# Graph layer on one core: routed groups 7 of 24 instead of 1 of 4, in seven slot tiles of two 64-row strips with 448 nodes each, and the loop written by groups

## The reference

```python
h = x @ W_in2f
Wij = ssp(f_ij @ W_filt1 + b_filt1) @ W_filt2 + b_filt2      # ssp(v) = softplus(v) - ln 2
x_ij = h[idx_j] * (Wij * rcut_ij[:, None])
agg = segment_sum(x_ij, idx_i, num_segments=6250)
out = layernorm(x + ssp(agg @ W_out1 + b_out1) @ W_out2 + b_out2)
```

## Time and profile before

| | us |
|---|---|
| runs shown: median (lowest to highest of 3) | 2651.81 (2647.66 to 2652.65) |
| profiled execution, its own time | 2648.1 |
| its span, first to last instruction | 2646.3 |
| around the span (difference of the two) | 1.8 |
| PE busy in the span | 2360.8 (89%) |
| POOL busy | 1906.8 (72%) |
| DVE busy | 1684.8 (64%) |
| ACT busy | 1597.0 (60%) |

### The profile page before, as it was taken

How to read it: one execution, slowest core, us unless ns; L and a number is a source line. 1 busy time by engine, 2 the same in 40 slices (tenths; PEclk the granted TensorE clock), 3 DMA queues, 4 the chain that set the end, 5 groups by cost and what they waited for, 6 DMA issues and landing times.

```text
span 2646.3 us, 59597 instructions
## 1 busy us (share of the span) xinstructions
PE 2360.8 (89%) x16274; PEld 1665.8 (63%) x16274; DVE 1684.8 (64%) x3700; ACT 1597.0 (60%) x3509; POOL 1906.8 (72%) x1208
## 2 busy tenths in 40 slices
PE   3678999899899999899898999999898999999978
PEld 3456666666666666666666666666666666666645
DVE  6466666566666666666665666666676666666637
ACT  1466666666665656656566656656566656656503
POOL 1378877777777777777777777777777777767821
PEclk8599999999999999999999999999999999999989
DMA  7566655556565655665565556555555555556524
GB/s 272 147 130 94 90 92 88 85 87 87 81 91 79 90 86 84 90 85 84 86 89 79 89 82 89 90 79 90 90 86 80 91 80 89 92 77 89 68 70 135
DMA packets 356079, 248.75 MB, mean 94 GB/s; under 512 B 89739, under 2 KB 329846, under 8 KB 355514
## 3 DMA queue, kind: packets, MB, share of 16 engines
q0 software_dynamic: 169200, 77.08, 30.5%
q1 hardware_dynamic: 181362, 153.75, 25.2%
q10 hardware_dynamic: 5148, 13.49, 1.3%
HBM read 148.41 MB, written 95.76 MB: 92 GB/s over the span
## 4 chain that ended last, share of the span: by engine, by line
PE 38%; DMA 25%; issue 16%; POOL 10%; ACT 6%; DVE 3%; POOLq 1%; ACTq 0%; SPq 0%; DVEq 0%
DMA table<-total,index 24%; PE unit_psum L1398 15%; POOL table L640 10%; PE unit_psum L1384 6%; PE both_psum L1345 5%; PE pre_psum L1335 4%; PE total_psum L1359 3%; PE both_psum L1369 2%; ACT soft L753 1%; ACT h_dst L775 1%; ACT soft L751 1%; PE both_psum L1341 1%; ACT ring L797 1%; PE pre_psum L1497 1%; DMA x_t<-in_x_t 0%
## 5 line engine op out<-in xcount | busy, mean ns | idle before, releaser
L640 POOL DMA_INDIRECT table<-total,index x1175 | 1878.9, 1599 | 628.3 <-issue 281.3
L1398 PE MATMUL unit_psum<-scat_hot,ring 128*128 128x348 bf16 x5238 | 833.7, 317 | 13.1 <-DVE scat_hot L1137 13.0
L775 ACT ACTIVATE h_dst<-both_psum,cols 128x128 f32<-128x128 f32 x1564 | 445.2, 369 | 500.9 <-PE both_psum L1369 471.5
L1398 PEld LDWEIGHTS unit_psum<-scat_hot,ring 128*128 128x128 bf16 x5238 | 512.5, 99 | 276.6 <-issue 13.5
L1384 PE MATMUL unit_psum<-moving,route_hot 128*128 128x386 bf16 x2328 | 434.0, 328 | 133.5 <-ACT ring L797 115.0
L1066 DVE SCALAR_TENSOR_TENSOR hidden<-pre_psum,soft 128x1024 f32<-128x1024 f32 x196 | 239.9, 1224 | 389.8 <-ACT soft L755 329.4
L1345 PEld LDWEIGHTS both_psum<-w_f,hidden 128*128 128x128 f32 x3128 | 420.8, 195 | 33.1 <-issue 0.2
L1345 PE MATMUL both_psum<-w_f,hidden 128*128 128x128 f32 x3128 | 422.3, 279 | 0.0
L1384 PEld LDWEIGHTS unit_psum<-moving,route_hot 128*128 128x128 bf16 x2328 | 211.5, 98 | 270.9 <-ACT ring L797 130.9
L760 ACT ACTIVATE total<-total_psum 128x516 f32<-128x516 f32 x294 | 178.2, 606 | 308.8 <-DMA table<-total,index 226.3
L1147 DVE TENSOR_TENSOR acc_t<-acc_t,unit_psum 128x348 f32<-128x348 f32 x306 | 157.4, 514 | 255.7 <-PE unit_psum L1398 235.5
(11 more groups left out here) (115 smaller groups left out, 1672.3 us busy)
## 6 DMA issues: line engine op xcount, KB each, us to landing
dst_b<-dst SPq DMA_DIRECT2D x391, 128.0 KB
src_b<-src SPq DMA_DIRECT2D x295, 128.0 KB, 6.4
f_t<-in_f_t SPq DMA_DIRECT2D x98, 256.0 KB
table<-total,index POOLq DMA_INDIRECT x1175
window<-h_parts SPq DMA_DIRECT2D x391, 32.0 KB
table<-zeros ACTq DMA_DIRECT2D x15, 640.0 KB, 4.4
parts<-table SPq DMA_DIRECT2D x36, 256.0 KB, 3.2
h_parts<-h_out SPq DMA_DIRECT2D x12, 384.0 KB, 4.0
```

What stands on the lines that cost most here:

```text
L640: pool.indirect_dma_start(tables[table], bass.IndirectOffsetOnAxis(index[:, i, k:k + 1], 0), total[:, i, k, 0:DIM], None, compute_op=ALU.a ...
L775: last = act.activation(h_dst[:, b, d], source, ACT.Copy, scale=cols[:, q[1] % COL_BUFFERS, weight:weight + 1])
L1398: last = pe.matmul(unit_psum[:, unit_bank(q, c), 0:SLICE], ring[:, r % RING, b, part * DIM:(part + 1) * DIM], scat_hot[:, r % RING, c * SL ...
```

## The change

Routing: 7 of 24 groups are routed (places 3, 6, 10, 13, 17, 20 and 23 of each unit of 24), and none of the last 7. There are 14 buckets of 448 nodes. A slot tile holds two buckets, one in rows 0 to 63 and one in rows 64 to 127 (strips), and there are 7 slot tiles and a ring of 7. `add_up` multiplies each strip by itself: 64 rows against 448 columns, strip 0 into one PSUM bank and strip 1 into the other, in turn. Each interval between two routed groups (3 or 4 groups) takes one slot tile's turn. The loop is written by groups: 48 groups written out, a hardware loop with 24 groups in its body (14 turns), the last 7 groups with 4 closing steps, into which the last slices are put. ACT's softplus is cut in three calls put at different places of two steps, the columns of a half unit (12 groups) are copied at once, `same` and `message` have three buffers instead of two. `place_routed` has 14 rounds instead of 6 and its own input. In the last stage the nodes of a chunk lie one per partition and row of 512 B (`(t p)` for `(p t)`), so `acc_t` is read without a stride. `zeros` and `x_rows` share space, and `x_rows` is loaded after the tables are zeroed.

```diff
-UNROLL = 6
-FIRST = 2 * UNROLL
+UNIT = 24
+ROUTED_AT = (3, 6, 10, 13, 17, 20, 23)
+PER_UNIT = len(ROUTED_AT)
+PEELED = 2
-BUCKETS, SLICES, SLICE = 6, 3, 348
-BUCKET = SLICES * SLICE
-SLOT_ROWS = BUCKETS * P
+STRIPS = 2
+STRIP = P // STRIPS
+SLOT_TILES = 7
+BUCKETS = STRIPS * SLOT_TILES
+BUCKET = 448
+SLOT_ROWS = SLOT_TILES * P
-RING = BUCKETS
+RING = SLOT_TILES
...
-        def run_quads(eng, step):
-            for i in range(-1, FIRST):
+        def run_groups(eng, step):
+            for i in range(-2, PEELED * UNIT):
                 step((0, i))
             with eng.Fori(0, LOOPS) as j:
-                for i in range(UNROLL):
-                    step((j, FIRST + i))
-            for i in range(FIRST + UNROLL * LOOPS, QUADS + 1):
+                for i in range(PEELED * UNIT, (PEELED + 1) * UNIT):
+                    step((j, i))
+            for i in range(LAST_UNIT, GROUPS + 4):
                 step((0, i))
...
+            def add_up(m, k, groups, part):
+                for r in part:
+                    pe.wait_ge(hot_done, through_hots(m, len(groups) - 1 - groups.index(r)))
+                    for p in range(3):
+                        first, final = r == groups[0] and p == 0, r == groups[-1] and p == 2
+                        for strip in range(STRIPS):
+                            rows = slice(strip * STRIP, (strip + 1) * STRIP)
+                            last = pe.matmul(unit_psum[:, strip, 0:BUCKET],
+                                             ring[rows, r % RING, k, p * DIM:(p + 1) * DIM],
+                                             scat_hot[rows, r % RING, :], start=first, stop=final)
...
+            def step_narrow(g):
+                m, j, groups = interval(g)
+                routing = j >= 0 and routes(plus(m, -1))
+                if exists(g):
+                    second_layer(g)
+                if j == 1:
+                    add_slices(m, False)
+                if routing and groups == 3 and j == 2:
+                    route(m, 2)
+                if routing and groups == 4 and j == 2:
+                    route(m, 0)
+                if routing and groups == 4 and j == 3:
+                    route(m, 4)
+                if g[1] % 2 == 0 and exists(plus(g, 2)):
+                    first_layer(pair_of(plus(g, 2)))
+                if routing and groups == 3 and j == 2:
+                    route(m, 3)
+                if exists(plus(g, -1)) and plain(g[1] - 1):
+                    sum_repeated(plus(g, -1), plain)
+                if j == 0:
+                    add_slices(m, True)
...
+                if exists(plus(g, 1)):
+                    gather(plus(g, 1))
...
+                if m[1] == ROUTES and j >= 4:
+                    for e in range(2 * (j - 4), min(2 * (j - 4) + 2, SLOT_TILES)):
+                        last_slices(e)
...
-                                 .rearrange("(p t) d -> p t d", t=tiles)).then_inc(parts_loaded[b], 16)
+                                 .rearrange("(t p) d -> p t d", t=tiles)).then_inc(parts_loaded[b], 16)
...
-                    acc = acc_t[:, bass.ds(chunk_number(c) * CHUNK, n)].rearrange("d (p k) -> d k p", k=tiles)
-                    pe.matmul(pre_psum[:, b, 0:n].rearrange("f (k p) -> f k p", k=tiles), w_o1[:, :], acc,
+                    pe.matmul(pre_psum[:, b, 0:n], w_o1[:, :], acc_t[:, bass.ds(chunk_number(c) * CHUNK, n)],
                               start=True, stop=False)
```

More of the change, by code:

```diff
@@ L110, in table_of, with number, plus, routed @@
[L110 to L117, removed]
+def number(g):
+    return UNIT * g[0] + g[1]
+def plus(g, n):
+    return g[0], g[1] + n
+def routed(i):
+    return 0 <= i < LAST_UNIT and i % UNIT in ROUTED_AT
+def plain(i):
+    return i >= 0 and not routed(i)
+def every(i):
+    return i >= 0
+def through(g, kind=every):
+    return sum(map(kind, range(UNIT))) * g[0] + sum(map(kind, range(g[1] + 1)))
@@ new lines, in last_before, with exists, is_at, pair_of @@
+def last_before(g, kind, n=0):
+    for i in range(g[1] - 1, -1, -1):
+        if kind(i) and (n == 0 or (g[1] - i) % n == 0):
+            return g[0], i
+    return None
+def exists(g):
+    return not isinstance(g[0], int) or 0 <= g[1] < GROUPS
+def is_at(g, n):
+    return isinstance(g[0], int) and g[1] == n
+def pair_of(g):
+    return g[0], g[1] // 2
+def through_pair(pair):
+    return UNIT // 2 * pair[0] + (pair[1] + 1)
+def quad_landed(quad):
+    return 16 * (UNIT // QUAD // 2) * quad[0] + 16 * (quad[1] // 2 + 1)
@@ new lines, in quad_number, with through_half, table_adds, unit_adds @@
+def quad_number(quad):
+    return UNIT // QUAD * quad[0] + quad[1]
+def through_half(g):
+    return 2 * g[0] + g[1] // HALF + 1
+def table_adds(k, adds):
+    return (adds - k + TABLES - 1) // TABLES
+def unit_adds(g, kind, tile):
+    return TILES * sum(kind(i) for i in range(g[1] // UNIT * UNIT, g[1])) + tile
+def table_of(g, kind, tile):
+    return unit_adds(g, kind, tile) % TABLES
+def adds_before(g, kind, tile, k):
+    per_unit = table_adds(k, TILES * sum(map(kind, range(UNIT))))
+    return 16 * per_unit * g[0] + 16 * (g[1] // UNIT * per_unit + table_adds(k, unit_adds(g, kind, tile)))
@@ L130, in left_over @@
[L130 to L149, removed]
@@ L152, in unit_bank, with through_routed @@
[L152 to L177, removed]
+def through_routed(r):
+    return PER_UNIT * r[0] + (r[1] + 1)
@@ L312, in build @@
[L312 to L328, removed]
+        weight_c = at(6528, "weight_c", [P, SLOTS * TILES], F32)
@@ L1388, in add_up @@
-            def add_up(q, c, b, olds, newest):
-                for r in (*olds, *newest):
-                    if c == 0:
-                        missing = 0 if r in newest else len(newest)
-                        if not isinstance(q[0], int) or after_hot(q, missing) > 0:
-                            pe.wait_ge(hot_done, after_hot(q, missing))
-                    for part in range(3):
-                        first = r == (*olds, *newest)[0] and part == 0
-                        final = r == (*olds, *newest)[-1] and part == 2
-                        last = pe.matmul(unit_psum[:, unit_bank(q, c), 0:SLICE],
-                                         ring[:, r % RING, b, part * DIM:(part + 1) * DIM],
-                                         scat_hot[:, r % RING, c * SLICE:(c + 1) * SLICE], start=first, stop=final)
-                last.then_inc(slice_mm_done, 1)
@@ L1487, in last_layers @@
                         pe.matmul(both_psum[:, b, d], half_sum[:, b, d], ident[:, :], start=True, stop=False)
-                        last = pe.matmul(both_psum[:, b, d], parts[:, b, 2, d], ident[:, :], start=False, stop=True)
+                        for table in range(2, TABLES):
+                            last = pe.matmul(both_psum[:, b, d], parts[:, b, table, d], ident[:, :], start=False,
+                                             stop=(table == TABLES - 1))
                     last.then_inc(e_agg_t, 1)
@@ L1545 @@
         "src_cols": columns(src_p),
+        "src_routed": columns(src_p.reshape(SLOTS, GROUP)[[g for g in range(LAST_UNIT) if g % UNIT in ROUTED_AT]]),
         "dst_cols": columns(dst_p),
```

1154 lines of the change are left out of this document (583 added, 571 removed).

## The result

The changed kernel takes 2881.31 us (median of 4 runs, 2874.62 to 2888.71) beside 2652.23 us for the kernel before (4 runs, 2647.66 to 2654.8): ratio 1.0866, 95% interval 1.0836 to 1.0897. The forecast was 2490 us, faster, with a range up to 2605. It was wrong in sign and by 391 us.

A forecast was written before the change was run, and what follows sets the result against it. PE was taken as the bound, with POOL 2% behind. Main stretch -146, start +14, last stage -22 and -8 sum to -162 us, giving 2490 us, range 2430 to 2605.

The forecast's parts named there:

- With the waits of today unchanged: PE, main loop: 123.0 us of work per 24 groups plus today's 15.1 us of waits and loop turns gives 138.
- main stretch: First scatter to last: 1114 scatters at 2.045 us, 2278 us for 2424, -146; ends 2172 and 2406.
- slower by waits in the new order on ACT or DVE: Lists of ACT and DVE: last_slices and copy_total block what stands behind them, making the kernel slower; some 3%.
- sign of being wrong: Main loop: forecast is wrong if scatters are over 2.10 us apart or POOL waits more for indices than now.
- PE's work: PE per 24 groups: 60.2 fixed, 32.5 routing and 30.3 slices, 123.0 us against 132.8.
- the ends: Slices on PE per 24 groups: 27.9 us with strips side by side, 55.9 in sequence; 30.3 taken.
- rival C: add_up on PE: strips run one after the other, 0.380 us per pair, time 2758 us; 7%.
- The rule on the tiling mode: Slices on PE: the skill says changing tiling mode drains TensorE; 0.17 us per visit was taken, 14 visits.
- 2.02 us per scatter, fed without a break: POOL, main loop: need per scatter without index waits; 68 scatters per 24 groups take 137.4 us.
- Start: Stage before the first scatter: 14 rounds of ranks for 6 and more bucket one-hots, +14 us; ends 0 and 17.
- one load more: Start stage: a further load ahead of the queue, behind the upper end of 17 us where +14 was taken.
- Last stage: Behind the last scatter: -22 us from last slices being covered, -8 from reading acc_t without stride against smaller load pieces.

The follow-up runs named there:

- e1: Changed kernel with finish_hidden moved ahead of the routing one-hots, compare_dst and make_index on DVE: 2802.99 us, ratio 1.053.
- e9: Kernel of e3 with all four routing one-hots made in one step on DVE, finish_hidden left in place: 2587.41 us, ratio 0.9759.
- e3: Changed kernel with both the moves of e1 and e2: 2701.35 us, ratio 1.0144.
- e4: Changed kernel with the two strips of a visit multiplied one after the other instead of in turn: 3416.92 us, ratio 1.2855.
- e10: Kernel of e5 with the edit of e4, strips one after the other: 2776.77 us, ratio 1.0485.
- e5: Kernel of e3 with finish_hidden and take_rest ahead of add_slices, four one-hots in one step, one ring eviction ahead of ACT's logarithm: 2509.38 us, ratio 0.9468.
- e2: Changed kernel with ACT's eviction of the ring's last slot tile moved to the front of its step: 2890.5 us, ratio 1.0862.

## Why the prediction was wrong

- **The step that failed**: "With the waits of today unchanged (6 x 1.69 + 5.0 = 15.1) that is 138". The idle time of PE went from 11.7 to 28.0 us per unit, and 6.7 us more went to the clock. The main stretch was to take 2.045 us per scatter and took 2663.9 / 1114 = 2.391. The waits belong to the order of the lists, which the change wrote anew on all engines, and today's number says nothing about a new order. The prediction named the mechanism only as "slower by waits in the new order on ACT or DVE", at 3%, and priced nothing of it. Its own sign of being wrong came true: scatters over 2.10 us apart and POOL waiting more for indices than before. The places stand in the new lists: `finish_hidden` behind `make_index` on DVE, the routing one-hots split over two steps, and `keep_slots` of 6 behind the logarithm; the moves of e1, e9 and e3 show that each held up PE. The list alone doesn't tell the price: in the kernel before, one of a quad's two `finish_hidden` stands behind two `make_index` as well, and PE waits for neither.
- **PE's work**: forecast 123.0 for 132.8 us per unit; by busy time less clock it is 127.7 for 134.9, so 7.2 of 9.8 came, give or take 1.5 for the two digits of the clock. The slices take 7 x (2.95 + 1.24) = 29.3 us, changes of mode inside the visits included, for the 30.3 forecast. Some 1 us of the missing 2.6 is in the steps beside the visits (next point); where the rest lies is open. Of the ends, 27.9 and 55.9, the first was nearly right, and by e4's visits the serial one would have been 7 x 6.67 = 46.7. With the strips in sequence and the order good, e10's 2777 us lie near rival C's 2758, but not by its sum, which had the visits 9 us per unit too long and no loss to the clock.
- **The rule on the tiling mode** (the Trainium skill, TensorEngine Tiling (Array Packing), Key Properties: a change of mode drains TensorE): each visit's change of mode costs little inside the visit, 2.95 - 15 x 0.190 = 0.10 us for the longer visit and 1.24 - 6 x 0.190 = 0.10 for the shorter, against 0.17 assumed. The steps beside it pay too: the second layer ahead of a short visit takes 0.99 us to the next start (1307.51 to 1308.50 in the changed kernel) for 0.89 in the earlier trace rows, and the sums behind one take 0.99 (1329.71 to 1330.70) for 0.90. So a short visit costs 0.3 us beyond its columns. Whether it is a drain no run shows.
- **POOL** at 2.02 us per scatter, fed without a break: e5 gives 2293.4 / 1114 = 2.059 with 56.8 us of waiting for an index, so 2.01 without. The forecast of 2.045 nearly holds once the order does.
- **Start**: +14 forecast, +18.0 measured. `place_routed` was sized rightly: on DVE it takes 29.3 us (32.19 to 61.46) for 14.9 (26.36 to 41.22), +14.4 for the +14.6 summed. Its rounds take 1.38 us (1.45 assumed) and its bucket one-hots 4.32 (4.6):

```profile
33.47 4.32 DVE L1038 TENSOR_SCALAR in_bucket<-bucket 128x448 bf16<-128x448 f32 x14
...
42.65 0.62 DVE L1061 TENSOR_TENSOR rank<-rank,rank_part 128x448 f32<-128x448 f32 x1
...
44.03 0.62 DVE L1061 TENSOR_TENSOR rank<-rank,rank_part 128x448 f32<-128x448 f32 x1
```

  What was missed lies ahead of it: the first load lands 6.3 us later and `place_routed` begins 5.8 us later, of which 2.3 are made up before the first scatter. The kernel before, then the changed one:

```profile
6.24 2.29 DVE L901 TENSOR_REDUCE dst_low<-dst_g 98x4 f32<-98x2048 int32 x1 [6.24 <-DMA dst_g<-in_dst]
```

```profile
12.52 2.29 DVE L972 TENSOR_REDUCE dst_low<-dst_g 102x4 f32<-102x2048 int32 x1 [12.52 <-DMA dst_g<-in_dst]
```

  The runs made from the changed kernel agree (24.07 us to PE's first matmul in e2 and 24.26 in e5, for 23.40 here and 17.52 in the kernel before). The prediction allowed 3 us for one load more; what delays the first load, no run shows.
- **Last stage**: -30 forecast, -26.4 measured. The last slices end ahead of the last scatter, and PE's first table work comes 13.8 us behind it, as said:

```profile
2778.88 1.31 PE L1452 MATMUL unit_psum<-scat_hot,ring 64*128 64x448 bf16 x12 [1.56 <-DVE scat_hot L1213]
...
2798.21 0.77 PE L1546 MATMUL both_psum<-ident,half_sum 128*128 128x128 f32 x2 [18.02 <-POOL half_sum L726]
```

  In the kernel before, PE's first table work came 36.9 us behind the last scatter, so this part gives 23.1 of the 22 forecast, and the rest, from PE's first table work to the end, 3.3 (83.1 to 79.8 us) of the 8. The multiplication of `acc_t` takes 0.86 us per chunk instead of 1.80, and PE is busy 63.3 us there for 70.8. The 256 KB load in 512 B pieces lands in 3.4 us (median), not 3.2, at the near end of the bounds. But PE now stands idle for 16.5 us for 12.3, 4.3 of them waiting for a table sum (1.6 in the kernel before), and the clock in this part is 0.89 for 0.93, at most 3 us. The two can explain the missing 4.7; that is argued, not tried.
- **The size of the loss**: 240 us against the -146 of the main stretch, a miss of 386, of which e5's order gives back 371 (2663.9 - 2293.4).

## What to carry over

When a change rewrites the order of in-order lists, the waits of the old order are no estimate for the new one. Walk each list through one period, note for each instruction that the bound engine waits for what stands ahead of it and what that waits for in turn, and give the case "the order couples the engines" a price and a real chance. If all engines get emptier and the time grows, repair the order before judging the design, and judge moves together: e2 alone looked worthless, and was worth 102 us beside e1.

## What the runs showed beyond that

Waits can cost twice, once for their length and once for the clock behind them. Behind a wait of 2.58 us the visit of 15 pairs took 4.70 us instead of 3.01, and behind one of 2.88 us the second layer took 1.92 instead of 1.05 (changed kernel, PE's timeline):

```profile
786.94 4.70 PE L1452 MATMUL unit_psum<-scat_hot,ring 64*128 64x448 bf16 x30 [2.58 <-ACT ring L848]
...
1333.97 0.61 PE L1398 MATMUL both_psum<-bias_f,ones_bias 96*128 96x512 bf16 x1 [2.88 <-DVE hidden L1140]
1334.37 1.92 PE L1402 MATMUL both_psum<-w_f,hidden 128*128 128x128 f32 x8
```

Not each wait does it: behind 2.61 us at 1304.11 the visit ran at the full level. Waits are not all of it: the mean clock is 0.956 in e5 and 0.927 in the changed kernel, which fits, but 0.932 in e10, which waits less than e5. There one visit took 9.86 us for 5.11 at a granted 0.50, some 3 us behind a gap of 3.98 us at a loop's turn; e5 has such gaps too. What the longer visits add to it is open. In turn on different halves of the array, one more pair of 64-row matmuls with 448 columns costs 0.190 us; strip by strip one more matmul costs 0.189 (e4). So the order of issue alone decides between one matmul's time for a pair and two.
